# Last layer of a four-layer network: in each VectorE slot the maxima of a turned pair move behind the scaling and the right taps

## The reference, cut to what matters

```python
h = bit_linear(x, w1)                                  # 512 -> 2048, ternary weights
h = depthwise_conv1d(h.transpose(0, 2, 1), conv_w, conv_b)   # 3 taps along the tokens
h = h.transpose(0, 2, 1)
h = jax.nn.silu(h)
return bit_linear(h, w2)                               # 2048 -> 512
# bit_linear rounds each token's row to int8 by 127 / max(abs(row)) before its product
x = x + jnp.tanh(g_ffn[1]) * _L1_ffn_ref(...)
```

## Time and profile before

| | |
|---|---|
| three timed runs | 1794.78, 1800.57 (median), 1801.24 us |
| profiled execution: time, span | 1798.3 us, 1796.5 us |
| PE busy | 1556.9 us (87% of the span) |
| DVE busy | 1276.3 us (71%) |
| ACT busy | 883.3 us (49%) |
| POOL busy | 574.0 us (32%) |

### The profile page before, as it was taken

How to read it: one execution, slowest core, us unless ns; L and a number is a source line. 1 busy time by engine, 2 the same in 40 slices (tenths; PEclk the granted TensorE clock), 3 DMA queues, 4 the chain that set the end, 5 groups by cost and what they waited for, 6 DMA issues and landing times. The chain is left out here.

```text
span 1796.5 us, 25689 instructions
## 1 busy us (share of the span) xinstructions
PE 1556.9 (87%) x9559; PEld 948.6 (53%) x9559; DVE 1276.3 (71%) x2065; ACT 883.3 (49%) x1430; POOL 574.0 (32%) x556
## 2 busy tenths in 40 slices
PE   6798888987678889878999998999996878888886
PEld 4444444443355658645666665666664534444443
DVE  5576778888443546744777776767766699999995
ACT  4455555555444336435334343343332577777763
POOL 3132343233210012123112111220200497777770
PEclk9899999999788889989999999999999899999999
DMA  5112221222723434521020110201011411111111
GB/s 167 41 48 95 94 72 47 72 71 94 281 77 96 165 103 141 192 101 48 1 83 24 59 60 25 72 34 59 13 47 36 180 62 65 65 65 65 53 48 47
DMA packets 73284, 142.34 MB, mean 79 GB/s; under 512 B 8418, under 2 KB 17782, under 8 KB 72907
## 3 DMA queue, kind: packets, MB, share of 16 engines
q1 hardware_dynamic: 71914, 137.55, 22.2%
q0 software_dynamic: 960, 3.15, 0.6%
q10 hardware_dynamic: 288, 0.00, 0.0%
HBM read 97.67 MB, written 43.01 MB: 78 GB/s over the span
## 5 line engine op out<-in xcount | busy, mean ns | idle before, releaser
L2859 POOL TENSOR_TENSOR E_y<-E_y,E_centre 128x1024 f32<-128x1024 f32 x64 | 151.6, 2369 | 10.4 <-ACT E_y L2888 8.2
L2774 PE MATMUL E_OP<-E_w2q,E_yb 128*128 128x512 bf16 x512 | 128.3, 408 | 25.2 <-issue 18.9
L1454 ACT ACTIVATE D_oT<-D_OB 128x512 fp32r<-128x512 f32 x64 | 38.3, 598 | 219.5 <-DVE D_OB L1771 219.5
L2851 POOL TENSOR_SCALAR E_centre<-E_hs,E_cw,E_cb 128x512 f32<-128x512 f32 x64 | 106.9, 1670 | 59.7 <-DVE E_hs L2941 59.4
L2764 PE MATMUL E_HP<-E_xT,E_w1q 128*128 128x512 bf16 x512 | 123.3, 385 | 0.4 <-ACT E_xT L2865 0.2
L1743 DVE TENSOR_TENSOR D_q_low<-D_PJ,D_q_high 128x512 fp32r<-128x512 f32 x60 | 41.5, 691 | 98.7 <-ACT D_q_high L1430 98.7
L2950 DVE SCALAR_TENSOR_TENSOR E_y<-E_hs,E_cw,E_y 128x512 f32<-128x512 f32 x128 | 104.5, 855 | 1.1 <-POOL E_y L2859 1.1
L2774 PEld LDWEIGHTS E_OP<-E_w2q,E_yb 128*128 128x128 bf16 x512 | 52.1, 104 | 94.5 <-issue 47.2
L1523 PE MATMUL D_PJ<-D_xT_high,D_wq_high 128*128 128x512 f32 x240 | 101.7, 424 | 0.1
L588 PE MATMUL A_TX<-A_wo,A_oT 128*128 128x512 f32 x176 | 90.9, 642 | 7.1 <-PEq L1106 7.1
L1523 PE MATMUL D_PJ<-D_xT_high,D_wq_low 128*128 128x512 f32 x240 | 94.9, 395 | 0.0
(11 more groups left out here) (427 smaller groups left out, 4130.0 us busy)
## 6 DMA issues: line engine op xcount, KB each, us to landing
A_res<-in_x SPq DMA_DIRECT2D x8, 1024.0 KB, 5.3
xn_d<-A_xn SPq DMA_DIRECT2D x8, 1024.0 KB, 4.7
x_d<-A_res SPq DMA_DIRECT2D x8, 1024.0 KB, 5.9
W_raw<-in_w1T SPq DMA_DIRECT2D x16, 512.0 KB, 3.6
W_raw<-in_w2T SPq DMA_DIRECT2D x16, 512.0 KB, 3.9
D_res<-x_d SPq DMA_DIRECT2D x8, 1024.0 KB, 6.1
x_d<-D_res SPq DMA_DIRECT2D x8, 1024.0 KB, 4.4
E_res<-x_d SPq DMA_DIRECT2D x8, 1024.0 KB, 5.4
```

The costliest lines, as they stand in the source:

```text
L2774: mm = pe.matmul(OP[:, :], yb[:, k, c * P:(c + 1) * P], w2q[:, k, :], start=k == 0, stop=k == MC - 1)
L2851: pool.tensor_scalar(U[i % 2][:, 0, :], hs[i % NBUF][:, 0, 1:TILE + 1], cw[:, 2 * p, 1:2], cb[:, 2 * p:2 * p + 1], ALU.mult, ALU.add).then ...
L2859: pool.tensor_tensor(y, y, U[i % 2][:, :, :], ALU.add).then_inc(t0, 1)
```

## The change

The first of the three steps of a DVE slot becomes the third. Nothing is added or removed, and no other engine's list changes.

```diff
             for n in range(STEPS + 2):
                 for p in range(MP):
                     i = MP * n + p
-                    if 0 <= i - FOLD < MP * STEPS:
-                        biggest(i - FOLD)
                     if n < STEPS and i > 0:
                         scale(n, p)
                     if 0 <= i - LAG < MP * STEPS:
                         right_taps(i - LAG)
+                    if 0 <= i - FOLD < MP * STEPS:
+                        biggest(i - FOLD)
                     if 1 <= n <= STEPS:
                         if p == FOLD - 1:
                             units(n - 1)
                         if p in QUANT:
                             quantise(n - 1, QUANT.index(p))
                     if p in ADD:
                         done = n - 1 if p == ADD[0] else n - 2
                         if 0 <= done < STEPS:
                             add_out(done, ADD.index(p))
```

## The result

The changed kernel takes 1827.57 us (median of four runs, 1817.78 to 1831.96) against 1800.02 for the kernel before (median of four): ratio 1.0151, 95% interval [1.0106, 1.0197]. It is slower, as forecast, but by 27.5 us instead of 16, above the forecast's range, which ends at 1823. The profiled execution took 1827.19 us, its span is 1825.4.

What follows compares the result with a forecast made beforehand. DVE's list plus its waits was taken to bound the kernel. From the profiled 1798.3 us, new waits at PE's present speed added 8.9 and PE's lower clock 8.8, giving 1816 us; the 8-in-10 range was 1803 to 1823.

Steps and rivals of the forecast that it cites:

- It leaves every instruction and its price as it is.: Whole kernel: only the times at which DVE's three steps run move; no instruction's duration changes, so 0 added.
- The cover: DVE work between maxima and add loses 2.47, so adds of c2, c3, c1 wait 1.81, 0.63, 1.28; tile +1.61.
- turning to projection: On PE, from the turning's start to the projection's start behind the maxima: taken as 1.04 us.
- chain: Maxima, turning, projection, out product, add: 7.79 us for c2 and c0, 8.23 for c1, 8.28 for c3.
- The units: DVE's units step, once a tile in the last layer: priced at 0.70 us, unchanged by the edit.
- 1.23 for slot 2's taps: DVE slot 2: taps take 2.64 against slot 1's 1.41; the extra lies inside c2's cover and changes nothing.
- The clock: PE idles 3.3 before c1's turning and returns slow: 1.25 per c1 add, seven adds, +8.8 us.
- nearest to the 1.67 that cost nothing: PE ahead of the turning for c0: an idle stretch of about 1.9 was expected to leave PE's speed alone.
- rival 4: PE's clock falls also behind idle stretches of 1.5 to 1.9 before turnings of slots 3, 5, 7: 1824; chance 0.07.
- Rival 2: Faster: PE gets from maxima to the adds of c2, c1, c3 in time, only gains remain: about 1788; chance 0.08.

Runs made afterwards that it cites:

- experiment 9: Changed kernel with extra PE matmuls ahead of the turnings of slots 1, 3, 5, 7, and POOL's long addition in halves: ratio 1.0069 to before, mean tile 45.37 us.
- experiment 3: Changed kernel with the units' small operation left out and extra PE matmuls ahead of the turnings of slots 1, 3, 5, 7: 1813.1 us, ratio 1.0056 to before.
- experiment 2: Changed kernel with 6 to 8 extra PE matmuls ahead of the turnings of slots 1, 3, 5, 7: 1817.7 us, ratio 1.0104 to before.
- Experiment 7: Kernel before with the maxima moved behind scaling and taps in slots 1, 3 and 7 alone: ratio 1.0231 to before, mean tile 48.16 us.
- experiment 6: Kernel before with the maxima moved behind scaling and taps in slots 0, 2, 4, 5 and 6: 1822.16 us, ratio 1.0125 to before.
- experiment 5: Kernel before with 14 extra PE matmuls ahead of c0's out product: ratio 0.9963 to before, mean tile 43.00 us.
- experiment 1: Changed kernel with the units' small operation (lower limit and factor) left out: ratio 1.0132 to before, mean tile 47.47 us.
- experiment 4: Kernel before with the maxima moved behind scaling and taps in slot 5 alone: 1797.57 us, ratio 0.9979 to before.

## Why the prediction was wrong

The direction, the mechanism and most terms held; the step that failed is the first sentence on what the change does: "It leaves every instruction and its price as it is." On DVE the price of the units' small operation rose from 0.37 to 1.83, a term that the sum put at nothing.

- *The cover.* Waits of 1.81, 0.63 and 1.28 were forecast for c2, c3 and c1, none for c0. With the clock held and the stall short (experiment 9) there are 1.82, none and 1.09; with the operation left out (experiment 3) c3 waits 0.25. The mean tile is then 45.37, +1.10 on 44.27, against +1.61 forecast. Part of the difference is a link that was too long: turning to projection is 0.90 (1621.80 to 1622.70) where I had taken 1.04 from one row. Held, a little too dear. In the changed kernel itself c3's 0.47 beside the forecast's 0.63 is luck: the stall lengthens c3's cover by 1.46 and the slow projection (3.24) its chain; with the clock held and the stall in place c3 waits for nothing (experiment 2). Experiment 7 shows that late maxima in slots 1, 3 and 7 are enough for the whole loss, experiment 6 that they are not the only way to lose.
- *The units.* Taken at 0.70 a tile with the rest of DVE's work. Their small operation takes 1.6 to 1.8 in seven tiles, because it now starts while POOL's addition runs. With the clock held that costs 46.46 - 45.37 = 1.09 a tile, some 8 us in seven tiles, an estimate. I had priced this very kind of meeting, 1.23 for slot 2's taps, and found that it lies inside c2's cover, but asked it of no other instruction. This is the failed step.
- *The clock.* Taken at 1.25 a tile at c1 alone. Keeping PE busy is worth 47.90 - 46.46 = 1.44 a tile, so the size was near. The places were in part wrong. At c1 the forecast came out where the idle stretch was its 3.3 (3.39, wait 2.62). But "nearest to the 1.67 that cost nothing" did not hold for the idle stretches of 1.93, behind which PE came back slow in some tiles, ahead of c3's and c0's out products too. That is rival 4's mechanism; where it struck ahead of c0's out product it shortened the idle stretch to 1.93 and so took c1's place (1.08 there) rather than adding to it.
- The three parts, 1.10, 1.09 and 1.44, make the 3.63 by which the mean tile grew; the forecast had 1.61, nothing and 1.25, together 2.86. The kernel before pays for the clock as well, 44.27 - 43.00 = 1.27 (experiment 5): with the clock held on both sides the new order without most of the stall costs 45.37 - 43.00 = 2.37, and the clock's share grows by 0.17 only. The parts are not independent: taken away alone, the stall gave 0.43 (experiment 1, with the operation itself), since a slow PE stood behind it.
- Rival 2 was excluded rightly: the adds of c1 and c2 do wait. Its gain exists, though, where the chain is not touched: slot 5 alone.

Two things remain open: why PE comes back slow behind some idle stretches of 1.93 and not behind others (in slot 7 this decides between tiles of 47.34 and 48.66), and the 1.70 ahead of the layer, which is within what the runs of one kernel differ.

## What to carry to other kernels

When a step moves by one place in an engine's list, ask of every instruction behind it, the smallest too, which instruction of which other engine runs at its new time; an operation on four numbers per partition took 1.8 us here. Find the loop that a moved step heads (here maxima, turning, projection, out product, add) and compare its length with the work left beside it. When two stalls lie in one stretch, removing either alone can show little: remove both, then each.

## What the runs showed of the hardware that was not expected

- The units' DVE operation on 128x4 ends only with the POOL instruction that is under way: 1.83 beside an addition of 2.36, 0.74 beside halves of 1.27, 0.37 beside the last of a product of 1.70, 0.17 with POOL idle. The reduction next to it, 0.19, ran while the same addition ran.
- Extra matmuls that nobody reads shorten the mean tile: 46.46 against 47.90 in the changed kernel, 43.00 against 44.27 in the kernel before, where the granted clock of a tile rose from 0.96 to 1.00 and the ratio is 0.9963 [0.9944, 0.9982].
- Idle stretches of PE of 1.93 were followed by the lower clock at 1610.1 and 1622.7, and by the full clock at 1634.3, in one tile. Idle stretches of 3.53 were followed by either as well, in experiment 4: by the lower clock at 1570.5 (0.50) and by the full clock at 1615.0 (1.00).
